# Attention maxima of two more head groups taken out of the QKV projection and into the attention's order of work

## The chip, the core and the metric

The kernel runs on one core of a Trainium2 chip. The metric is the device time of one execution in microseconds (us). A core has TensorE (PE: matmuls and transposes, PEld: its weight loads), VectorE (DVE), ScalarE (ACT), GpSimd (POOL) and SyncE (SP), each with its own queue of instructions worked off in order, and DMA queues: SP issues to the hardware queue, GpSimd to the software queue. TensorE writes to eight PSUM banks of 128 x 512 floats. Engines meet at semaphores only.

## What is computed

One "macaron" block on x of shape (1, 2048, 512): half a mixture-of-experts layer, attention, half a mixture-of-experts layer again, each with a layer norm ahead. The attention has 16 query heads and 4 key/value heads of 32, rotary positions and a causal mask:

```python
x = x + 0.5 * ffn(layernorm(x), router_w, w1, w2, w3)      # 8 experts, the best 2 of each token
x = x + attention(layernorm(x), wq, wk, wv, wo)
x = x + 0.5 * ffn(layernorm(x), router_w, w1, w2, w3)

# attention, per head
attn = where(mask, -inf, q @ k.T / sqrt(32))
out  = softmax(attn) @ v
```

The softmax here subtracts the true maximum of each row: the maximum of a query's scores over all keys that it may see has to be known before the scores are made, because it goes into the score matmul as two extra rows (96 and 97) of the query tensor `Qs`.

## The kernel before

**Stages.** First layer norm, router and experts (to about 260 us), the projection (to 414), the attention (to about 1018), then routing and experts of the second half (to 1282).

**Projection** (`project_plan` L1104, `pe_project` L1361, `dve_project` L1213, `act_project` L1298). 16 chunks `i` of 128 tokens. For a chunk, TensorE makes q, k and v (`qkv`, L1398: 24 matmuls for chunks 0 to 13, in three passes of split floats, 8 full-precision ones for the last two), transposes the next normed chunk (L1372), and transposes the rotated q and k of the chunk before into `Qs` and `Ks` (`stack`, L1415; copied by ScalarE, L1327). VectorE norms a chunk two ahead (L1228 to L1239), makes the low half of the split (L1245) and the rotation (`rope_split`, L1256 to L1271).

**Maxima.** Queries are worked on in 16 groups `G`: block `b = G // 4` of 512 queries, and four heads (`G % 4`). `tops_of(G)` (L987) lists a group's *maxima*: for each of its 4 heads and 4 times 128 queries, one per block of 512 keys up to its own block. `pe_top` (L991) makes the 128 x n scores in a PSUM bank (L997) and `dve_top` (L1001) takes the maximum of each row. For an earlier block that is one reduction over 512 columns ("full", L1010). For the own block it is `n = (c + 1) * 128` columns with the mask added ("masked", L1012). Groups 0 to 3 have 16 maxima each, all masked; groups 4 to 7 have 32, 8 to 11 48 and 12 to 15 64. The partial maxima lie in `PM`, which has room for two groups (`G % 2`).
When a group's maxima are there, a *solve* follows: VectorE reduces and splits them (`dve_found` L1017 in the projection, `dve_found_in_bank` L1034 in the attention, step "solvemax"), TensorE transposes them (`pe_found` L1053, L1059, step "found"), ScalarE copies the result to `mT` (`act_found` L1063, L1068, step "foundcopy"), and SP carries it to memory and back into rows 96 and 97 of `Qs` (`sp_found` L1084: `top<-mT` L1089, a wait for its landing, `Qs<-top` L1093). TensorE waits for that landing before the group's first score (L1628).

**Where the maxima stand.** `project_plan` puts those of groups 0 to 3 in between the projection's matmuls, from chunk 5 on: six in a chunk, four in chunk 15. Maxima, solves and stacks share a ring of three banks (5, 6, 7). VectorE reads a chunk's maxima ahead of that chunk's rotation.

**Attention** (`attend_plan` L1508). One list of steps, which every engine walks through and takes its own part of, sets the order. It runs over 160 tiles (group, 128 keys); a tile `n` has four scores `4n` to `4n + 3` (one per head, L1636), numbered 0 to 639, each followed by ScalarE's exp (L1755). Behind the last score of a tile comes the weighing of the tile before (L1648, and L1666 for the sums of exps that TensorE makes). GpSimd masks the tiles of the own block (L1814). For groups 8 and up, part of the sums of exps is made by GpSimd in `CH` (L1828) and by adding DMAs into `CD` (`CD<-P`, `CD<-CH`, L1844), which TensorE takes in at the group's end (L1657). Groups begin at scores 0, 16, 32, 48, 64, 96, 128, 160, 192, 240, 288, 336, 384, 448, 512 and 576.
The maxima of groups 4 to 15 are spread over the scores by weight: `weight` counts scores (a masked one by its share of columns), `given` counts maxima in the same measure, and maxima are put in while `given < 1.1 * weight`. A group's solve comes at the next tile end at which no sum is in the way.
Other steps stand at fixed distances from the end of a block: `xo` (SP loads the residual x, L1987), two steps `xoy` (GpSimd adds the experts' output to it by an adding DMA, `XO<-y`, L1861), and the finish of a block (projection by `WO` L1703, layer norm, store, router). They don't move with the maxima.

## Time and profile before

| | us |
|---|---|
| three runs | 1285.0, 1286.23, 1287.75 (median 1286.23) |
| the profiled execution | 1283.76 |
| its span, first to last instruction | 1282.5 |
| TensorE busy | 1197.2 (93%) |
| VectorE busy | 893.1 (70%) |
| ScalarE busy | 665.8 (52%) |
| GpSimd busy | 598.1 (47%) |

All times below are microseconds from the start of the profiled execution's span. An engine's busy time counts its own instructions, not its waits. In a timeline, the brackets at the end of a row give the idle time before the instruction and what ended it. The granted clock of TensorE is given as a share of 2.4 GHz.

### The profile page before, as it was taken

What the parts mean: (1) busy time and instruction counts of PE and PEld (TensorE: products, weight loads), DVE (VectorE), ACT (ScalarE), POOL (GpSimd) and SP (SyncE); (2) the same over time, 40 slices, a digit from 0 to 9 for tenths busy, and PEclk for the clock granted to TensorE, in tenths of its full rate; (3) what the DMA queues carried; (4) which work ended last, traced back from release to release, by engine and by line L of the source; (5) the groups of instructions that cost most, each with busy time, mean ns of one, the idle gap of its engine ahead of it and who ended that gap; (6) DMA issues with size and microseconds to landing.
All of it is one profiled execution on the core that took longest, in us unless ns stands there. A gap on an engine that the chain in (4) does not pass through costs nothing.

```text
span 1282.5 us, 22107 instructions
## 1 busy us (share of the span) xinstructions
PE 1197.2 (93%) x7413; PEld 778.6 (61%) x7413; DVE 893.1 (70%) x2100; ACT 665.8 (52%) x1321; POOL 598.1 (47%) x496
## 2 busy tenths in 40 slices
PE   4899999999998999999999999999999978999996
PEld 3678888858776554445545455545544346777774
DVE  7767777779997665476577677587763666666664
ACT  2545455436555554265466556366567853444442
POOL 4844444313210111001437556455773373888886
PEclk9899999999999999999999999999999999999999
DMA  9923333565530022013445845655743263666665
GB/s 331 365 92 108 112 111 108 172 178 108 98 60 16 21 69 35 1 59 78 98 127 138 165 100 106 192 133 146 152 100 67 84 240 72 106 100 102 101 102 79
DMA packets 68557, 148.52 MB, mean 116 GB/s; under 512 B 8832, under 2 KB 29312, under 8 KB 64448
## 3 DMA queue, kind: packets, MB, share of 16 engines
q0 software_dynamic: 35184, 93.34, 34.1%
q1 hardware_dynamic: 33264, 53.77, 12.1%
q8 instruction: 64, 1.05, 0.3%
q14 instruction: 45, 0.37, 0.1%
HBM read 81.28 MB, written 33.55 MB: 90 GB/s over the span
## 4 chain that ended last, share of the span: by engine, by line
PE 61%; DVE 15%; DMA 10%; issue 6%; POOL 4%; ACT 4%; SPq 0%; POOLq 0%; DVEq 0%; ACTq 0%
PE bank L839 10%; PE bank L1636 10%; PE bank L1648 9%; PE bank L997 8%; PE bank L862 5%; PE bank L1703 4%; PE bank L1666 4%; DMA XG<-xn,TK 3%; DMA out<-Y,DI 3%; POOL out L789 3%; DVE bank L1012 2%; DMA CD<-P 2%; DVE PM L1010 2%; PE bank L821 2%; PE bank L1398 2%
## 5 line engine op out<-in xcount | busy, mean ns | idle before, releaser
L1755 ACT ACTIVATE P<-bank 128x512 f32<-128x512 f32 (+3 forms) x640 | 304.2, 537 | 255.4 <-PE bank L1636 246.2
L1010 DVE TENSOR_REDUCE PM<-bank 128x1 f32<-128x512 f32 x384 | 252.9, 685 | 79.7 <-PE bank L997 78.9
L1636 PE MATMUL bank<-Qs,Ks 98*128 98x512 f32 (+3 forms) x640 | 242.8, 409 | 5.1 <-ACT P L1755 2.8
L997 PE MATMUL bank<-Ks,Qs 96*128 96x512 f32 (+3 forms) x640 | 233.4, 386 | 8.9 <-DVE PM L1012 5.3
L1636 PEld LDWEIGHTS bank<-Qs,Ks 98*128 98x128 f32 x640 | 117.2, 190 | 141.5 <-ACT P L1755 65.3
L1814 POOL TENSOR_SCALAR_AFFINE_SELECT P<-P 128x512 f32<-128x512 f32 x64 | 43.5, 694 | 283.4 <-ACT P L1755 283.4
L1012 DVE CUSTOM_DVE_ANT_0 bank<-bank,KB 128x128 f32<-128x128 f32 (+3 forms) x256 | 124.5, 497 | 51.4 <-PE bank L997 50.7
L1648 PE MATMUL bank<-P,V 128*32 128x512 f32 (+3 forms) x1280 | 151.3, 544 | 4.1 <-POOL P L1814 4.1
L997 PEld LDWEIGHTS bank<-Ks,Qs 96*128 96x128 f32 x640 | 121.7, 191 | 54.1 <-DVE PM L1010 17.0
L1828 POOL TENSOR_TENSOR CH<-CH,P 128x512 f32<-128x512 f32 x108 | 139.5, 1446 | 13.3 <-ACT P L1755 12.7
L789 POOL DMA_INDIRECT out<-Y,DI x78 | 126.3, 1619 | 38.2 <-issue 28.0
L951 DVE TENSOR_TENSOR DL<-W,DH 128x512 fp32r<-128x512 f32 x152 | 98.3, 688 | 41.0 <-issue 21.1
L766 POOL DMA_INDIRECT XG<-xn,TK x78 | 93.5, 1199 | 33.1 <-issue 18.0
L912 ACT CAST DH<-W 128x512 fp32r x152 | 86.7, 618 | 20.3 <-issue 20.3
L839 PE MATMUL bank<-WH,XH 128*128 x312 | 92.4, 418 | 0.9 <-issue 0.6
L839 PE MATMUL bank<-WL,XH 128*128 x312 | 85.7, 396 | 1.5 <-DVE XL L933 1.5
L839 PE MATMUL bank<-WH,XL 128*128 x312 | 85.4, 395 | 0.0
L778 POOL DMA_INDIRECT y<-Y,DI x39 | 38.7, 993 | 96.4 <-DVE Y L961 96.4
L933 DVE TENSOR_TENSOR XL<-bank,XH 128x512 fp32r<-128x512 f32 x78 | 53.9, 691 | 32.8 <-ACT XH L892 28.4
L898 ACT ACTIVATE G<-bank 128x256 f32<-128x256 f32 x78 | 29.9, 384 | 85.0 <-PE bank L839 85.0
L892 ACT CAST XH<-bank 128x512 fp32r<-128x512 f32 x78 | 45.8, 587 | 45.2 <-PE bank L821 42.1
L839 PEld LDWEIGHTS bank<-WL,XH 128*128 128x128 f32 x312 | 58.6, 188 | 16.1 <-issue 1.9
(195 smaller groups left out, 1977.7 us busy)
## 6 DMA issues: line engine op xcount, KB each, us to landing
CD<-P POOLq DMA_DIRECT2D x17, 1024.0 KB, 7.3
xn<-XN SPq DMA_DIRECT2D x8, 1024.0 KB, 6.9
WR<-L_ffn_w POOLq DMA_DIRECT2D x16, 512.0 KB, 15.1
XO<-y POOLq DMA_DIRECT2D x8, 1024.0 KB, 9.6
WR<-L_ffn_w SPq DMA_DIRECT2D x16, 512.0 KB, 7.7
CD<-P SPq DMA_DIRECT2D x7, 1024.0 KB, 5.2
CD<-CH POOLq DMA_DIRECT2D x7, 1024.0 KB, 7.5
XA<-y POOLq DMA_DIRECT2D x24, 256.0 KB, 4.1
```

Of the source, the lines that this page charges most:

```text
L766: pool.indirect_dma_start(out=x.XG[:, j % NG, :], out_offset=None, in_=g.xnd[f][:, :], in_offset=bass.IndirectOffsetOnAxis(ap=r.TK[:, j:j ...
L789: pool.indirect_dma_start(out=g.out.rearrange("t (h d) -> (t h) d", h=2), out_offset=bass.IndirectOffsetOnAxis(ap=r.DI2[:, h, j:j + 1], ax ...
L839: ins = pe.matmul(bk(g, 2 + j % 2), part[:, k * P:k * P + P], w[:, bass.ds(ev[j] * 2048 + k * 512, 512)], start=(n == 0 and k == 0), stop= ...
L912: act.copy(x.DH[:, k, :], W.W3[:, bass.ds(e * 1024 + k * 512, 512)]).then_inc(s("dh"), 1)
L951: ins = dve.tensor_tensor(x.DL[:, k, :], W.W3[:, bass.ds(e * 1024 + k * 512, 512)], DHf[:, k, :], ALU.subtract)
L997: pe.matmul(bk(g, bank)[:, 0:n], g.Qs[b][0:96, G % 4 * 4 + h, c * P:c * P + P], g.Ks[0:96, G % 4, k * BQ:k * BQ + n], start=True, stop=Tru ...
L1010: dve.tensor_reduce(dst, bk(g, bank)[:, 0:n], AX.X, ALU.max).then_inc(s(f"free{bank}"), 1)
L1012: dve.tensor_tensor_reduce(out=bk(g, bank)[:, 0:n], in0=bk(g, bank)[:, 0:n], in1=g.KB[:, CB_MASK + BQ - n:CB_MASK + BQ], scale=1.0, scalar ...
L1636: pe.matmul(bk(g, bank)[:, o:BQ], g.Ks[0:98, G % 4, k * P:k * P + P], g.Qs[G // 4][0:98, G % 4 * 4 + j, o:BQ], start=True, stop=True).then ...
L1648: ins = pe.matmul(bk(g, 3)[32 * h:32 * h + 32, o:BQ], g.V[:, k, q * HD:q * HD + HD], a.P4[buffer_of(n)][:, h, o:BQ], start=(k == 0), stop= ...
L1755: act.activation(a.P4[buffer_of(n)][:, j, o:BQ], bk(g, score_bank(g, i))[:, o:BQ], ACT.Exp, scale=scale).then_inc(s("exp"), 1)
L1828: ins = pool.tensor_tensor(to[:, h, :], two[:, h, :], one[:, h, :], ALU.add)
```

## The change

The maxima of groups 2 and 3 leave the projection: `EARLY = 2` groups are made there, three maxima per chunk (two in chunk 15) at every fourth part of its matmuls in place of every eighth. In the attention the list of maxima starts with group 2, and the spread becomes `given < 1.15 * weight + 6`: 1.15 per score, with six in advance. An assertion in the planner makes sure that a group's maxima don't overwrite the partial maxima of the group two before. Everything else stays.

```diff
+EARLY = 2
@@ project_plan
-    ahead = [key for G in range(4) for key in tops_of(G)]
+    ahead = [key for G in range(EARLY) for key in tops_of(G)]
@@
-                if (total - done) % (total // 8) == 0 and done > total // 4 and i > 4 and ahead:
+                if (total - done) % (total // 4) == 0 and done > total // 4 and i > 4 and ahead:
@@
-        if told < (64 - len(ahead)) // 16:
+        if told < (16 * EARLY - len(ahead)) // 16:
@@
-    assert told == 4
-    g.shared = [("found", G) for G in range(4)]
+    assert told == EARLY
+    g.shared = [("found", G) for G in range(EARLY)]
@@ attend_plan
-    ahead = [key for G in range(4, 4 * NB) for key in tops_of(G)]
+    ahead = [key for G in range(EARLY, 4 * NB) for key in tops_of(G)]
@@
-    told, weight, given, extra, known, solved, turned, free = 4, 0.0, 0.0, [], [], [], [], True
+    told, weight, given, extra, known, solved, turned, free = EARLY, 0.0, 0.0, [], [], [], [], True
@@
-            while ahead and given < 1.1 * weight:
+            while ahead and given < 1.15 * weight + 6:
                 key = ahead.pop(0)
+                assert key[1] < EARLY + 2 or ("solvemax", key[1] - 2) in plan, key
```

## Rows read from the trace of the kernel before

**Rows 1.** Busy time by stretch: bounds, length, then each engine's; clock; DMA.

```profile
301.50:308.45 6.95, 6.95 (x51) 6.22 (x50) 6.70 (x17) 4.52 (x12) 2.84 (x3) 1.00 0.54 105
308.45:316.41 7.96, 7.96 (x57) 6.97 (x55) 7.25 (x26) 4.51 (x12) 2.84 (x3) 1.00 0.61 116
308.45:390.28 81.83, 75.79 (x502) 64.33 (x500) 78.92 (x251) 43.27 (x95) 15.07 (x17) 1.00 0.44 80
467.40:927.08 459.68, 447.78 (x2981) 234.57 (x2977) 317.82 (x796) 245.03 (x499) 192.89 (x181) 0.99 0.47 111
710.07:713.49 3.42, 3.41 (x19) 1.35 (x20) 0.00 (x0) 0.18 (x1) 0.44 (x1) 0.50 1.12 182
```

**Rows 2.** Timeline of VectorE: start, length, instruction; a chunk, and the attention's first.

```profile
343.22 0.82 DVE L1256 TENSOR_TENSOR t<-bank,cs 128x640 f32<-128x640 f32 x1
...
348.41 0.29 DVE L1012 CUSTOM_DVE_ANT_0 bank<-bank,KB 128x128 f32<-128x128 f32 x1
...
350.88 0.69 DVE L1228 BATCH_NORM_STATS2 stA<-XA 128x6 f32<-128x512 f32 x1
...
351.93 0.82 DVE L1256 TENSOR_TENSOR t<-bank,cs 128x640 f32<-128x640 f32 x1
...
415.18 0.69 DVE L1010 TENSOR_REDUCE PM<-bank 128x1 f32<-128x512 f32 x1 [4.59 <-PE bank L997]
```

**Rows 3.** Timeline of TensorE in the attention, at six places.

```profile
422.34 0.28 PE L1636 MATMUL bank<-Qs,Ks 98*128 98x256 f32 x1
...
611.37 0.50 PE L1636 MATMUL bank<-Qs,Ks 98*128 98x512 f32 x1
...
710.08 1.51 PE L1648 MATMUL bank<-P,V 128*32 128x384 f32 x8 [1.81 <-POOL P L1814]
...
731.74 0.40 PE L997 MATMUL bank<-Ks,Qs 96*128 96x512 f32 x1
731.97 0.40 PE L1636 MATMUL bank<-Qs,Ks 98*128 98x512 f32 x1
...
734.79 0.60 PE L1059 MATMUL bank<-K,M 128*8 128x128 f32 x4
...
979.06 1.06 PE L1657 MATMUL bank<-CD,ones 128*32 128x512 f32 x8 [0.50 <-DMA CD<-CH]
```

**Rows 4.** Timeline of SP's issues to the hardware queue.

```profile
652.17 0.27 SPq L1089 DMA_DIRECT2D top<-mT  x1
656.45 0.22 SPq L1093 DMA_DIRECT2D Qs<-top  x1
...
681.42 0.38 SPq L362 DMA_DIRECT2D xn<-XN  x1
...
692.22 0.29 SPq L1089 DMA_DIRECT2D top<-mT  x1
693.68 0.25 SPq L1093 DMA_DIRECT2D Qs<-top  x1
694.03 0.39 SPq L1987 DMA_DIRECT2D XO<-L_attn_x  x1
...
906.57 0.29 SPq L1089 DMA_DIRECT2D top<-mT  x1
911.78 0.24 SPq L1093 DMA_DIRECT2D Qs<-top  x1
```

**Rows 5.** Timeline of GpSimd's issues to the software queue.

```profile
606.58 1.29 POOL L1861 DMA_DIRECT2D XO<-y  x1 [0.43 <-issue]
...
649.32 0.87 POOL L1844 DMA_DIRECT2D CD<-P  x1 [4.89 <-ACT P L1755]
...
707.10 0.86 POOL L1844 DMA_DIRECT2D CD<-CH  x1 [4.34 <-DMA CD<-P]
...
903.87 2.09 POOL L1861 DMA_DIRECT2D XO<-y  x1
```

**Rows 6.** Chain of the work that ended last, in order of time: start, length, what.

```profile
693.93 12.63 DMA CD<-P
```

## Prediction

> **What bounds the kernel now.** I read the stretches of time first, because the change takes work out of one stage (the projection, up to 414 us) and puts it into another (the attention, 414 to 1018 us), so what counts is what each stage is short of. A chunk of the projection without a maximum takes 6.95 us, and TensorE is busy for all of it; the first chunk with six maxima takes 7.96 us, again with TensorE full [rows 1]. The nine chunks with six maxima together take 81.83 us, or 9.09 each, but there TensorE is busy for only 75.79 us of it and VectorE for 78.92: the later of these chunks are VectorE's [rows 1]. The timeline of VectorE confirms it: from one chunk's first rotation product (343.22) to the next one's (351.93) are 8.71 us without an idle time, of which six maxima take 350.88 - 348.41 = 2.47 us [rows 2]. Without them VectorE's own chunk is 6.24 us, less than TensorE's 6.95. In the attention the roles are turned: from 467.40 to 927.08 TensorE is busy for 447.78 of 459.68 us, VectorE for 317.82 [rows 1]. So a maximum that leaves the projection gives back VectorE time that was on the path, and in the attention it costs TensorE time that is on the path. Last I looked at what is not steady: transfers and waits around the attention's groups, in the timelines of SP and GpSimd [rows 4, 5], since the new plan moves every later group's maxima by some scores.
>
> **Projection, what is removed.** 32 of 64 maxima go (groups 2 and 3, all masked ones, of 128 to 512 columns), and two of the four small solves that end a group's maxima. Three per chunk stay in place of six. TensorE's price of one, from the first chunk, where nothing waits: (7.96 - 6.95) / 6 = 0.17 us [rows 1]. VectorE's price: 2.47 / 6 = 0.41 us for the six narrower ones of that chunk [rows 2]; over all four widths I take 0.44, an estimate. A chunk then needs 6.95 + 3 x 0.17 = 7.46 us of TensorE and 6.24 + 3 x 0.44 = 7.56 us of VectorE, so both are nearly equal and I take 7.56. Nine chunks make 68.0 us, plus 0.5 for the one solve that still falls in them: 68.5 in place of 81.83, a gain of 13.3. The last two chunks lose three and two maxima, 5 x 0.17 = 0.8. Together **-14.1 us**. From both sides: if the two engines wait for each other now and then, and a chunk takes 7.8, the gain is 12; if VectorE's surplus is carried along to the end and TensorE sets 7.46, it is 15. The tail of the stage (the last rotation, its transposes) has the same instructions as before.
>
> **Attention, what is added.** The planner's arithmetic, followed, gives 28 maxima between scores 0 and 15 (14 before), 16, 13 and 15 in the next three groups (14, 13, 14), 24 more than before in groups 4 to 13 (15 full ones, 9 masked), and 28 in place of 36 in group 14; the last is placed after score 533, not 541.
> Group 0: twelve maxima stand behind score 0, and 24 behind the first eight scores. TensorE can be only three banks ahead of VectorE, so VectorE sets the pace: from 415.18 [rows 2], 24 x 0.44 = 10.6 us, to 425.8; then the small solve (0.6) and its transposes, 0.60 by their row at 734.79 [rows 3], so that score 9 starts at 427.0 where it started at 422.34 [rows 3]. That is +4.6. The half clock with which the attention starts lies under VectorE's work then.
> Groups 1 to 3: one full maximum fewer and four masked more, and one solve more. A full one costs TensorE 731.97 - 731.74 = 0.23 us in the steady part [rows 3]; for a masked one I take 0.19, between the projection's 0.17 and that. A solve costs up to 0.60 of transposes, partly overlapped, and something of a wait for VectorE's three small operations; I take 0.8 in all (0.4 to 1.2). Sum +1.3.
> Groups 4 to 13: 15 x 0.23 + 9 x 0.19 = +5.2. VectorE has the room (317.82 of 459.68 us busy [rows 1]), so I add nothing for it; the bound above is 24 x 0.44 = 10.6.
> Group 14: eight maxima fewer would be worth 1.8 us, but the transfer that carries GpSimd's share of the sums already comes last there: TensorE waited 0.50 us for it at 979.06 [rows 3]. Its chain starts with exps of this group that the change moves by a few tenths. I count nothing back (-1.8 to +0.4) and take +0.3.
> Sum of the four: 4.6 + 1.3 + 5.2 + 0.3 = **+11.4 us**, 8 to 15.
>
> **Attention, what is moved.** Two pieces hang on the order of the queues. *Group 8's maxima.* Their copy by ScalarE and their two small transfers (to memory and back into Qs) stood behind score 177 and now stand behind score 185; group 8's first score is 192, at 611.37 [rows 3]. GpSimd's adding transfer of the residual (the second XO<-y of block 1) stands behind score 185 as well, just ahead, and was issued at 606.58 [rows 5]. A small transfer behind such a one waits for it: issued at 652.17 behind CD<-P of 649.32 it let the second go only at 656.45, and issued at 906.57 behind XO<-y of 903.87 only at 911.78; with nothing in the way the step takes 693.68 - 692.22 = 1.46 us [rows 4, 5]. In both loaded cases the step ended 7.1 and 7.9 us after the large one's issue. So for group 8: 606.58 + 7.1 to 7.9 = 613.7 to 614.5, and one more step of 1.46: 615.1 to 616.0. TensorE stands before score 192 until then, 3.8 to 4.6 us, and all that it has queued (scores, maxima, weighing) stands behind it, with ScalarE and VectorE waiting. After an idle 1.81 us at 710.08 the clock stood at half for 3.42 us [rows 1, 3], so I add 1.5 for the clock: **+5.7 us** (0 to 8). The other groups keep time: group 4 is the next tightest, seven scores for some 3.5 us of copy and transfers.
> The Trainium skill (DMA: Bandwidth & Descriptors, Queues, rings and completion order) says that an engine takes turns between queues packet by packet, draining a whole packet before it switches. By that rule a small transfer would wait for a part of the large one only; if that part is short, the term falls to about nothing and the sum to some 1280.5. The rows above show waits of 2.8 and 3.8 us.
> *Block 2's residual.* SP took the transfers of group 10's maxima (behind score 265) ahead of the load XO<-L_attn_x (behind 266); now that copy stands behind 269 and the load goes first. The load doesn't wait for a score, so it leaves right behind the store of XN, issued at 681.42, and not at 694.03 [rows 4]. There it ran together with CD<-P of 693.93, which took 12.63 us [rows 6]; GpSimd waited 4.34 us for it at 707.10 [rows 5], the mask behind it came late, TensorE idled 1.81 us at 710.08 [rows 3] and had the half clock until 713.49 [rows 1]. Without the collision that is 1.81 + about 1.4 (3.42 us at half speed, partly spent on work that waits anyway) = **-3.2 us**. The load then meets the CD<-P ahead of that one, issued about when XN is stored; nobody needs it before the next is issued at 693.93, so I count no new wait (up to +2).
>
> **Sum.** -14.1 + 11.4 + 5.7 - 3.2 = -0.2 us. The profiled execution took 1283.76 us (span 1282.5 and 1.3 around it), so 1283.6 by this; the median of the three runs is 1286.23, 2.5 above it, so the forecast is 1286.0.
>
> **The rivals.**
> *1. Group 8's maxima land in time* (faster). The small transfers get through between the packets, or GpSimd's large one leaves later than they do. For it: the margin is decided by which of two issues, some 2 us apart, comes first. Against: both loaded cases, with 2.85 and 2.70 us between the two issues [rows 4, 5]. Time: 1286.0 - 5.7 = 1280.3.
> *2. The collision moves but doesn't go* (slower). The residual's load, now right behind the store of XN (681.42 [rows 4]), lies on top of that and of the CD<-P of the same moment; if that CD<-P takes over 12 us too, an exp that needs its buffer and the next CD<-P wait for it, and the -3.2 turns into +1 or so: 1290.2. It decides from a landing later than 693.93 on. For it: three megabytes at once. Against: two at once took 12.63 us [rows 6], and half a microsecond less than that is still in time; the store also begins first.
> *3. The burst costs more* (slower). With TensorE waiting for VectorE in the first 10 us, its clock may stay at half beyond them, and groups 0 to 3 lose 2 to 3 us more: 1288.5.
> *4. The maxima hide in the attention* (faster). Steps in which TensorE waits for ScalarE could take some of the 24 masked or full ones; by a third of 11.4: 1282.2.
> That the change doesn't do what it says I leave out: every maximum is in a list, and both lists come from the same function.
>
> **How the numbers follow.** A measurement of this kernel tells about 0.2% from no change, 2.6 us. Forecast 0.40 (1283.5 to 1288.8), rival 1 0.22, rival 2 0.16, rival 3 0.12, rival 4 0.10. Faster by over 0.2% (below 1283.6): rivals 1 and 4 and a little of the forecast, 0.34. Slower (above 1288.8): rivals 2, most of 3, and a little of the forecast, 0.28. Same 0.38. The range reaches to rivals 1 and 2 with the projection's bounds: 1280.0 to 1291.5.
>
> **What the new profile would show.** Chunks of 7.5 to 7.6 us in the projection, the first score near 400; group 0 some 4.5 us longer, with TensorE waiting for PM; an idle time of 4 us before the score that opens group 8, with a top<-mT whose second half leaves late; no idle time at the mask in group 9, and XO<-L_attn_x issued right behind xn<-XN; the rest, from the experts on, unchanged. I am wrong if a projection chunk stays above 8 us, or if the attention grows by less than 9 or more than 20 us.

## The result, and the profile after

The changed kernel takes 1299.02 us (median of four runs, 1297.82 to 1300.71), the kernel before on the same chip 1285.62 (four runs, 1283.95 to 1287.75): a ratio of 1.010, 95% interval 1.007 to 1.013. It is slower by 13 us. The forecast was 1286.0, the range ended at 1291.5, and slower had the smallest of the three chances. The profiled execution took 1298.21 us, with a span of 1297.0; before it was 1283.76 and 1282.5.

Each run below has a label, e1 to e15. The table holds the lengths of the stages of all runs below, read from the starts of the first projection matmul, of the scores that open a group, and of score 639. "G4-6" is groups 4 to 6 together. What lies after score 639 (the last tile and the second half's experts) has the same work in all of them, and took between 269.1 and 274.1 us in the profiled executions, in no order that follows the edits; so single steps are judged by the stages, and a kernel by its interval.

```
                     projection   G0  G1-3   G4-6  G7-8    G9  G10-13   G14   G15  attention
before                    140.4  12.2  40.9  109.9  87.4  50.3   212.1  49.9  36.4   599.1
after                     127.0  21.7  42.2  112.3  97.6  48.6   214.7  51.1  36.4   624.5
e1_ramp                   125.9  16.2  44.3  112.4  99.0  50.0   215.1  52.2  36.0   625.3
e2_late_add               125.8  21.8  42.2  112.4  90.5  48.5   214.7  51.1  36.3   617.5
e3_warm                   125.7  21.9  42.2  114.0  96.0  48.5   214.7  52.4  36.0   625.6
e4_before_load_first      141.8  11.2  40.9  109.9  87.4  47.3   212.2  49.9  36.5   595.2
e5_ramp_late_add          125.7  18.5  44.3  112.4  90.6  48.4   214.7  51.1  36.3   616.3
e6_fill                   125.7  18.4  42.2  112.4  96.7  48.5   214.6  52.4  36.0   621.2
e7_xo_back                127.1  21.8  42.2  113.9  96.1  47.2   214.6  51.1  36.5   623.4
e8_before_spread          140.4  17.5  40.8  110.1  90.2  47.1   214.6  48.9  36.4   605.5
e9_all                    125.7  16.1  44.3  112.4  90.6  47.4   214.7  52.3  36.0   613.8
e10_three_early           134.7  17.0  41.4  113.6  90.6  48.9   213.9  50.4  36.3   612.0
e11_pe_twice              127.2  21.5  42.8  113.8  92.1  48.7   217.6  52.4  37.2   626.2
e12_dve_twice             127.0  21.5  44.4  122.0  93.3  50.4   222.7  51.8  36.3   642.4
e13_dve_short             125.7  21.7  42.1  110.1  89.9  48.4   213.1  50.9  36.3   612.4
e14_both_short            126.9  21.5  42.0  109.4  88.9  50.0   211.5  50.9  36.5   610.5
e15_load_first_again      140.4  12.2  40.9  109.9  87.4  47.1   212.1  49.9  36.5   596.0
```

The projection gave back 13.4 us, near the 14.1 of the sum, and the attention took 25.4 where the sum had 13.9. The stretches of the changed kernel that answer to [rows 1] (bounds, length, busy time of PE, PEld, DVE, ACT, POOL, granted clock, DMA share, GB/s) are a chunk without a maximum, the first with three, the nine, the attention up to score 9, the first 9.4 us of group 8, and groups 4 to 13:

```profile
303.58:310.49 6.91, 6.91 (x52) 6.20 (x49) 6.66 (x17) 4.51 (x12) 2.83 (x3) 1.00 0.55 109
310.49:317.84 7.35, 7.35 (x55) 6.61 (x52) 5.97 (x20) 4.50 (x12) 2.84 (x3) 1.00 0.64 119
310.49:378.44 67.95, 67.73 (x467) 59.98 (x465) 64.53 (x190) 42.93 (x93) 15.30 (x17) 1.00 0.52 95
402.95:419.48 16.53, 15.67 (x54) 9.39 (x54) 12.05 (x51) 4.51 (x9) 1.27 (x2) 0.59 0.18 65
617.50:626.90 9.40, 9.40 (x37) 6.86 (x38) 5.97 (x13) 5.85 (x10) 0.00 (x0) 0.50 0.28 112
466.85:940.00 473.15, 453.92 (x3004) 240.68 (x3000) 329.05 (x828) 247.29 (x499) 192.71 (x181) 0.99 0.46 108
```

The nine chunks took 67.95 us, 7.55 each, with TensorE busy for all but 0.22: VectorE, at 64.53 us, is no longer what sets them. The two other short stretches stand out by the clock: 0.59 and 0.50, where 0.50 is its lower level, 1.2 GHz. TensorE's timeline shows what they consist of (start, length, instruction, idle time before it and what ended that):

```profile
404.07 0.71 PE L998 MATMUL bank<-Ks,Qs 96*128 96x512 f32 x2 [0.24 <-DVE PM L1013]
...
415.45 1.94 PE L1650 MATMUL bank<-P,V 128*32 128x512 f32 x8
417.16 1.81 PE L1668 MATMUL bank<-P,ones 128*32 128x512 f32 x8
...
419.12 0.60 PE L1060 MATMUL bank<-K,M 128*8 128x128 f32 x4
...
617.50 0.80 PE L1638 MATMUL bank<-Qs,Ks 98*128 98x512 f32 x1 [4.09 <-DMA Qs<-top]
...
709.66 0.50 PE L998 MATMUL bank<-Ks,Qs 96*128 96x512 f32 x1 [1.53 <-ACT mT L1069]
```

In the first stretch, the weighing and the sums at 415.45 and 417.16 take nearly twice as long as the same instructions at full speed (1.06 and 1.07 us in group 14 of the kernel before). At 617.50 stands the idle time that the prediction had put at 3.8 to 4.6 us. The one at 709.66, in group 9, it had not. VectorE in the burst, its first two rounds of four masked maxima and its last:

```profile
403.66 0.30 DVE L1013 CUSTOM_DVE_ANT_0 bank<-bank,KB 128x128 f32<-128x128 f32 x1 [5.76 <-PE bank L998]
...
405.43 0.33 DVE L1013 CUSTOM_DVE_ANT_0 bank<-bank,KB 128x128 f32<-128x128 f32 x1
...
407.48 0.33 DVE L1013 CUSTOM_DVE_ANT_0 bank<-bank,KB 128x128 f32<-128x128 f32 x1
...
416.26 0.22 DVE L1044 TENSOR_REDUCE bank<-PM 128x16 f32<-128x16 f32 x1
```

The first round takes 405.43 - 403.66 = 1.77 us, 0.44 for each maximum as forecast. The second takes 2.05, since now VectorE waits for TensorE at times too: 24 maxima took 416.26 - 403.66 = 12.6 us, not 10.6.

### The profile page after: what moved, and what is told of

It is laid out like the page before. It is cut to its first block, busy times and chain, and to the rows that moved or that the text cites. A ratio compares the mean times of both kernels' runs of the same rounds, so it can differ in the third digit from the quotient of the medians.

```text
span 1297.0 us, 22109 instructions
## 1 busy us (share of the span) xinstructions
PE 1209.3 (93%) x7413; PEld 787.1 (61%) x7413; DVE 890.7 (69%) x2100; ACT 669.3 (52%) x1321; POOL 597.5 (46%) x496
## 3 DMA queue, kind: packets, MB, share of 16 engines
q1 hardware_dynamic: 33264, 53.77, 12.2%
## 4 chain that ended last, share of the span: by engine, by line
PE 63%; DVE 13%; DMA 10%; issue 6%; POOL 5%; ACT 3%; SPq 0%; POOLq 0%; DVEq 0%; ACTq 0%
PE bank L840 10%; PE bank L1638 9%; PE bank L998 8%; PE bank L1650 8%; PE bank L863 6%; PE bank L1705 4%; PE bank L1668 4%; DMA out<-Y,DI 3%; PE bank L1399 3%; DMA XG<-xn,TK 3%; DVE PM L1011 3%; POOL out L790 3%; PE bank L822 2%; DVE bank L1013 2%; PE bank L1416 2%
## 5 line engine op out<-in xcount | busy, mean ns | idle before, releaser
L998 PEld LDWEIGHTS bank<-Ks,Qs 96*128 96x128 f32 x640 | 124.3, 195 | 50.5 <-DVE PM L1011 16.3
L1830 POOL TENSOR_TENSOR CH<-CH,P 128x512 f32<-128x512 f32 x108 | 139.2, 1440 | 13.4 <-ACT P L1757 12.8
L790 POOL DMA_INDIRECT out<-Y,DI x78 | 125.7, 1612 | 39.3 <-issue 29.4
L1668 PE MATMUL bank<-P,ones 128*32 128x512 f32 (+3 forms) x664 | 67.2, 476 | 2.4 <-DVE PM L1011 2.1
## 6 DMA issues: line engine op xcount, KB each, us to landing
WR<-L_ffn_w POOLq DMA_DIRECT2D x16, 512.0 KB, 14.5
```

The source lines that it names most:

```text
L790: pool.indirect_dma_start(out=g.out.rearrange("t (h d) -> (t h) d", h=2), out_offset=bass.IndirectOffsetOnAxis(ap=r.DI2[:, h, j:j + 1], ax ...
L998: pe.matmul(bk(g, bank)[:, 0:n], g.Qs[b][0:96, G % 4 * 4 + h, c * P:c * P + P], g.Ks[0:96, G % 4, k * BQ:k * BQ + n], start=True, stop=Tru ...
L1668: ins = pe.matmul(bk(g, 4)[32 * h:32 * h + 32, o:BQ], g.ones[:], a.P4[buffer_of(n)][:, h, o:BQ], start=fresh, stop=last)
L1830: ins = pool.tensor_tensor(to[:, h, :], two[:, h, :], one[:, h, :], ALU.add)
```

## Group 8: the transfer behind the adding DMA

SP's issues, then GpSimd's, around the opening of group 8 in the changed kernel:

```profile
610.33 0.29 SPq L1090 DMA_DIRECT2D top<-mT  x1
615.39 0.25 SPq L1094 DMA_DIRECT2D Qs<-top  x1
```

```profile
607.94 1.29 POOL L1863 DMA_DIRECT2D XO<-y  x1 [0.43 <-issue]
```

The small transfer left 2.39 us behind the adding one and its step took 5.06 us, as in the loaded cases of [rows 4, 5]. The experiment takes the adding transfer out of its way:

```diff
-        put(at + 22, ("xoy", b, 1))
+        put(at + (32 if b == 1 else 22), ("xoy", b, 1))
```

> The changed kernel, but the second XO<-y of block 1 stands ten scores later (195 in place of 185), behind the transfers of group 8's maxima. Theory 1 (that adding transfer holds the small ones up): top<-mT takes 1.5 us and not 5.07, the idle 4.09 us before group 8 goes and the half clock of 10.24 us with it, and groups 7 and 8 take 97.6 less 8 to 9 us. Theory 2 (seven scores are too few for copy and transfers anyway, or the clock falls there for another reason): at least 1.5 us of idle time or a half clock stays, and the gain is below 5.

It took 1291.31 us, a ratio to the kernel before of 1.0016 (0.9992 to 1.0040). Its SP issues, then GpSimd's:

```profile
607.75 0.29 SPq L1090 DMA_DIRECT2D top<-mT  x1
609.21 0.25 SPq L1094 DMA_DIRECT2D Qs<-top  x1
```

```profile
611.28 1.29 POOL L1863 DMA_DIRECT2D XO<-y  x1 [0.43 <-issue]
```

TensorE's row of score 192 there:

```profile
611.04 0.50 PE L1638 MATMUL bank<-Qs,Ks 98*128 98x512 f32 x1 [0.20 <-DMA Qs<-top]
```

The step takes 1.46 us, TensorE is idle for only 0.20 us before score 192 and keeps full speed, and groups 7 and 8 take 90.5 us in place of 97.6: theory 1, though it had 8 to 9 us. So this wait cost **7.1 us**: 4.09 of idle time before group 8, and the rest, by subtraction, from the half clock that came with it, 10.2 us long. In four other runs with the same wait (3.7 to 4.3 us) that half clock lasted 6.8 (e3, e6, e7) or 13.7 us (e1), and group 8 took 58.0, 58.1, 57.9 and 60.5 us against 59.3 here: 3.4 us of half clock more or less went with 1.2 us.

## Group 0: the burst and the clock

Four experiments on the changed kernel and one on the kernel before. **e1** builds the advance up slowly, and e5 adds the later adding transfer to it:

```diff
-            while ahead and given < 1.15 * weight + 6:
+            while ahead and given < 1.15 * weight + min(6, at / 8):
```

> The changed kernel, but its six maxima in advance are given out over the first 48 scores (min(6, score / 8) in place of 6); from there on its plan is the same. Theory 1 (the burst at the attention's start leaves TensorE waiting for VectorE, and its clock stays at half): the half clock of 13.65 us shrinks to 3.4 to 7, and groups 0 and 1 take 31 to 33 us in place of 36.6, so the kernel gains about 4 to 5. Theory 2 (the moved maxima themselves are dear, wherever they stand): groups 0 and 1 stay within 1 us of 36.6 apart from the five maxima that leave group 0 for groups 1 and 2.

> The changed kernel with both repairs: the advance of six maxima is only built up over the first 48 scores (min(6, at / 8)), and block 1's second adding transfer of the residual is put behind score 202 in place of 185 (the copy of group 8's maxima stands behind 185 or later). Nothing is left out. Theory 1 (the two causes are separate and add up): group 0 16 us and groups 0 to 3 together 60.5 (63.9 in the changed kernel), groups 7 and 8 together 90.5 (97.6), no idle time before the score that opens group 8; the attention 624.5 - 3.4 - 7.1 = 614, the kernel some 10 us under the changed one, 1288 to 1290, so within 0.3% of the kernel before. Theory 2 (what is taken away comes back further on, since the plan's maxima are only moved): the attention stays above 618 and the time above 1292.

**e3** puts 12 products that nobody reads ahead of the last transposes of the projection, where TensorE waits for the last rotation:

```diff
     def stack(i):
+        if i == NT - 1:
+            for _ in range(12):
+                pe.matmul(bk(g, 4), g.KB[:, CB_ONE:CB_ONE + P], g.KB[:, 0:512], start=True, stop=True)
```

> The changed kernel with twelve idle matmuls into bank 4 while TensorE waits for the last rotation (2.67 us), ahead of the projection's last transposes. Theory 1 (the idle time before the attention sets the clock down, and the burst only keeps it there): no half clock between 398 and 419, the last transposes take 2.6 us in place of 4.05, group 0 takes 15 to 17 us in place of 21.7, total gain 5 to 7. Theory 2 (the burst's waits for VectorE set the clock down by themselves): the transposes gain 1.5 us, and group 0 still shows a half clock of several us and stays above 19.

**e6** puts such a product into the burst itself:

```diff
             pe_top(g, step)
+            if step[1] == 2:
+                pe.matmul(bk(g, 4), g.KB[:, CB_ONE:CB_ONE + P], g.KB[:, 0:512], start=True, stop=True)
```

> The changed kernel, with one more product of 512 columns behind each of group 2's 16 maxima, written to a bank of the sums that the first weighing overwrites; nothing is left out. In group 0 TensorE then does work where it waited for VectorE. Theory 1 (TensorE's clock stands at half in the burst because it waits for VectorE there; the clock is the price above VectorE's own 24 x 0.44 us): the half clock of 13.7 us from 405 on shrinks to under 7 us, the burst keeps VectorE's pace, the weighing and the sums behind it run at full clock (about 1.0 us in place of 1.9 each), and group 0 takes 19 to 20 us in place of 21.7, in spite of the added products. Theory 2 (the clock falls whatever TensorE does there, or the added products take longer than the waits that they fill): the half clock stays at 10 us or more and group 0 takes 22 us or more.

**e8** is the kernel before with the new spread alone (`given < 1.15 * weight + 6` in place of `given < 1.1 * weight`):

> The kernel before, with the new spread alone: its 36 maxima of groups 4 on are still spread after four groups were told in the projection, but by 1.15 per score with six in advance (18 maxima behind the first eight scores in place of 10, 22 in group 0 in place of 14; group 8's copy stands behind score 169, well ahead of the adding transfer at 185). Nothing is left out. Theory 1 (the burst itself costs, by VectorE's pace and by the clock that falls with it): the half clock after score 0 lasts 10 us or more in place of 3.4, group 0 takes 16 to 17.5 us in place of 12.2, where eight more full maxima at 0.25 us would give 14.2. Group 8 has no idle time ahead of it and takes 53 to 54 us. The kernel is 5 to 10 us slower than before, about half of it given back in group 14, which has 6 maxima in place of 36. Theory 2 (the burst needs masked maxima of moved groups to hurt, or costs by its count alone): group 0 at 14.2 us or less and the half clock at 3.4 us.

Stretches from score 0 on: e6 up to score 9 and up to group 1, then group 0 of e1, of e5, and of e8, each from its own trace:

```profile
398.83:412.02 13.19, 13.00 (x69) 7.27 (x70) 11.47 (x51) 4.32 (x9) 1.27 (x2) 1.00 0.25 81
398.83:417.19 18.36, 17.59 (x112) 9.70 (x112) 13.63 (x59) 6.95 (x17) 2.46 (x4) 1.00 0.19 60
```

```profile
398.77:414.94 16.17, 14.78 (x91) 8.14 (x91) 11.21 (x49) 7.01 (x17) 2.55 (x4) 0.89 0.22 67
```

```profile
399.62:418.14 18.52, 17.49 (x91) 9.86 (x91) 11.58 (x49) 7.17 (x17) 2.55 (x4) 0.72 0.19 59
```

```profile
414.53:432.02 17.49, 16.94 (x87) 10.27 (x87) 12.11 (x33) 6.65 (x16) 2.47 (x4) 0.71 0.18 61
```

- e6: with TensorE given work in its waits, the clock stays at 1.00, though 16 products are added. Score 9 comes 13.19 us behind score 0; in the changed kernel it comes after 16.53, and the prediction had 12.7. The 24 maxima take VectorE 10.98 us there, where the prediction had 10.6 and the changed kernel 12.6. So of the burst's excess **3.3 us is the clock's**, and VectorE's pace was forecast nearly right. (1294.65 us, 1.0076, 1.0044 to 1.0107.)
- e3: work ahead of the projection's last wait doesn't help. The half clock came just the same, from 401.9 for 13.7 us, and group 0 took 21.9: it is in the burst that TensorE has to have work. (1300.3 us, two runs.)
- e1 and e5 have the same plan in group 0, and 16.17 and 18.52 us. The difference is the half clock alone: 3.4 us long in one and 10.2 in the other. Why it lasted longer in one, these runs don't show. What the slower advance saves in group 0 it gives back in part in groups 1 to 3 (44.3 for 42.2 us). e1 took 1298.67 us (1.0079, 1.0021 to 1.0138): its 3.4 us in groups 0 to 3 went again in groups 7 and 8 (half clock 13.7 us and not 10.2), in group 9 (3.4 us of half clock that the changed kernel's trace doesn't have), and in group 14, where TensorE waited 2.62 us for GpSimd's mask and the changed kernel 0.72. e5 took 1291.11 us (1.0045, 1.0026 to 1.0064), its attention 616.3 us where theory 1 said 614; the 2.3 missing are group 0's clock.
- e8: the new spread alone makes group 0 of the kernel before 5.3 us longer, with the half clock at 10.2 in place of 3.4 us, and the kernel takes 1295.22 us (1.0071, 1.0048 to 1.0094). The new spread is a cost of its own, without a single maximum moved out of the projection: the attention takes 605.5 us for 599.1. Part of the 5.3 us is the work of eight more maxima in group 0, four full and four masked (the expectation took eight full ones, at 2 us). Group 8 took 55.2 us, not the 53 to 54 expected. Group 14, with 6 maxima in place of 36, gave back only 1.1 us, not the half that was expected: there GpSimd's additions set the end (below). With group 10's copy at score 253 there, its group 9 takes 47.1 us, without the wait at the mask too.

## Group 9: block 2's residual

Undone in the changed kernel (e7), and done alone in the kernel before (e4, and e15 with more rounds):

```diff
-        put(at, ("xo", b))
+        put(at + (4 if b == 2 else 0), ("xo", b))    # e7, on the changed kernel
+        put(at - (4 if b == 2 else 0), ("xo", b))    # e4 and e15, on the kernel before
```

> The kernel before with nothing changed but the place of block 2's residual load: four scores earlier (262), so that SP issues it ahead of the transfers of group 10's maxima. Theory 1 (it only moves the collision): the idle 1.81 us at the mask and the half clock at 710 go (-3.2), the CD<-P that is issued with the store of XN takes 13 to 14 us and holds up an exp and TensorE by about 2.3, so group 9 takes 49 to 50 us in place of 50.3. Theory 2 (as I predicted: a free gain): group 9 takes 47 us.

> The kernel before with block 2's load of the residual four scores earlier, the same as in the earlier run, to tell 0.2%. Nothing is left out. Theory 1 (its trace's gain of 3 us in group 9 is a gain of the kernel): 1283 to 1285 where the kernel before has 1286 to 1287, a ratio of 0.997 to 0.999. Theory 2 (executions differ by as much in their experts' stage): a ratio of 0.999 to 1.001.

> The changed kernel with block 2's load of the residual put four scores later, so that the two small transfers of group 10's maxima go ahead of it again, as in the kernel before. Nothing is left out. Theory 1 (the queue order of this load sets what group 9 waits for): the idle time of 1.5 us ahead of the score that opens the last tile of group 9 goes, CD<-P and the load run together a step later, TensorE waits 1.5 to 2 us at the mask of tile 280 and the half clock comes back for 3.4 us there; group 9 takes 50 to 52 us in place of 48.6, and the kernel is 1.5 to 3 us slower than the changed one. Theory 2 (the collision's place doesn't matter to group 9): group 9 stays within 48.3 to 49.0 us and the time is the same.

In the kernel before, the load ahead of the small transfers shortens group 9 from 50.3 to 47.3 and 47.1 us, the 3.2 of the sum (theory 2 of e4); the kernel as a whole gives 1285.6 (1.0002, 0.9975 to 1.0029) and 1284.36 us against 1288.27 (0.9984, 0.9960 to 1.0007). That is a gain in the trace and none that the times can tell from no change. In the changed kernel the same order costs: e7, with the load behind again, has a *shorter* group 9 (47.2 for 48.6 us), and no wait at the mask. Its SP issues, then those of the changed kernel, and then a part of the changed kernel's chain of the work that ended last (start, length, what):

```profile
691.31 0.38 SPq L363 DMA_DIRECT2D xn<-XN  x1
705.52 0.29 SPq L1090 DMA_DIRECT2D top<-mT  x1
709.95 0.25 SPq L1094 DMA_DIRECT2D Qs<-top  x1
710.30 0.40 SPq L1989 DMA_DIRECT2D XO<-L_attn_x  x1
```

```profile
693.97 0.38 SPq L363 DMA_DIRECT2D xn<-XN  x1
694.46 0.44 SPq L1989 DMA_DIRECT2D XO<-L_attn_x  x1
```

```profile
694.07 13.91 DMA CD<-P
...
708.08 0.07 ACT P L1757
...
708.58 0.59 ACT P L1757
709.17 0.45 ACT mT L1069
709.62 0.04 issue
709.66 0.50 PE bank L998
```

The load did meet the CD<-P ahead of the critical one, as the prediction said; but that one then took 13.91 us, ScalarE's exp waited for its buffer, and behind the exp on ScalarE's queue stood the copy `mT` for which TensorE waits. In e7 the load leaves at 710.30, and no CD<-P near it is waited for. Neither theory of e7 held (the first had the sign wrong, the second no change). The collision's first place costs 1.4 us here, and its second, where the kernel before lost 3, is empty in the new plan since the copy has moved from score 265 to 269. The kernel as a whole took 1296.66 us (1.0095, 1.0059 to 1.0132).

That the order on ScalarE's queue makes the difference shows in e4, which has the same collision. ScalarE's rows there:

```profile
691.27 0.56 ACT L1068 CAST mT<-bank 8x512 fp32r<-8x512 f32 x1
...
695.25 1.08 ACT L1755 ACTIVATE P<-bank 128x512 f32<-128x512 f32 x2 [1.97 <-DMA CD<-P]
```

An exp waits for a CD<-P there too, 1.97 us, but `mT` was copied 4 us ahead of it, and TensorE lost nothing. In e2, which has the changed kernel's order, the wait for `mT` is there again (1.56 us at 700.01).

## What a maximum costs the attention

Groups 4 to 13 got 23 maxima more, 14 full and 9 masked (508 in the trace, 485 before; the prediction counted 24). Without group 8's wait (e2) they are 466.08 us long, where before they had 459.68, and group 9 had lost its 3 us of wait on the way: so 6.4 + 3.1 = 9.5 us for 23 maxima and what they disturb (1.4 of it the new wait in group 9), not 5.2. Four runs price TensorE's and VectorE's part apart; all have the later adding transfer, so e2 is what they are held against. The same 48 full maxima, four in each of groups 4 to 15, are made twice by one engine, or over 128 of their 512 columns:

```diff
+    if k == 0 and c == 0 and b:      # e11: the product twice
+        pe.matmul(bk(g, bank)[:, 0:n], ..., start=True, stop=True)
```
```diff
+        if k == 0 and c == 0:        # e12: the reduction twice
+            dve.tensor_reduce(dst, bk(g, bank)[:, 0:n], AX.X, ALU.max).then_inc(g.dv.sem, 1)
+            dve.wait_ge(g.dv.sem, g.dv.up())
```
```diff
-        dve.tensor_reduce(dst, bk(g, bank)[:, 0:n], AX.X, ALU.max)...     # e13; e14 cuts the product too
+        dve.tensor_reduce(dst, bk(g, bank)[:, 0:(P if k == 0 and c == 0 else n)], AX.X, ALU.max)...
```

> The changed kernel with the later adding transfer (as in the run that had only that), where TensorE makes 48 of the full maxima's products twice, four in each of groups 4 to 15, into the same bank; VectorE has nothing more to do. Nothing is left out. Theory 1 (a maximum's place in the attention costs TensorE's 0.23 us and that is all on the path): 48 x 0.23 = 11.0 us more attention than without the doubling (617.5), 628 to 629. Theory 2 (steps in which TensorE waits take some of it): 4 to 9 us more.

> The same 48 maxima, but VectorE reduces each of them twice (and waits for its own first one); TensorE has nothing more to do. Nothing is left out. It adds some 48 x 0.75 = 36 us of VectorE work between 430 and 960 us. Theory 1 (VectorE has the room, as the prediction had it): 0 to 3 us more attention than without the doubling (617.5). Theory 2 (VectorE's part of a maximum reaches the path where its work is bunched, which is why a moved maximum cost 0.33 us and not 0.22): 4 to 10 us more, spread over the groups, with the most in those that have row statistics.

> The changed kernel with the later adding transfer, in which VectorE reduces only 128 of the 512 columns of 48 full maxima, the same four in each of groups 4 to 15 that were doubled before; TensorE makes them whole. Left out is the maximum over the other 384 columns of these. It takes some 48 x 0.4 = 19 us from VectorE and nothing from TensorE. Theory 1 (VectorE's part of a maximum is on the path already at its present size, where its work is bunched): the attention 3 to 10 us under 617.5. Theory 2 (VectorE has room as it is, and only the 36 us added before went beyond it): 0 to 2 us under.

> The same, and the product of these 48 maxima is made over 128 columns only as well. Left out is the same part of the maxima, with its products. It takes 48 x 0.17 = 8 us from TensorE beside VectorE's 19. Theory 1 (both are on the path, in turn): the attention another 5 to 8 us under the run with the short reduction alone, 10 to 16 in all. Theory 2 (TensorE alone sets it): 6 to 9 us under 617.5 in all, and all of it from this step.

Attention against e2's 617.5 us: e11 +8.7 (1300.8 us in all), e12 +24.9 (1316.27), e13 -5.1 (1286.63), e14 -7.0 (1284.77; -8.5 without the 1.5 that a half clock at 695.6 put back into group 9).

- e11: a doubled product costs 0.18 us (theory 2, not the 0.23 of the sum).
- e12: a doubled reduction costs 0.52, far above both theories. It is 0.69 us long and waits for its twin. Part of the 0.52 is the clock: this trace has 20.5 us of half clock in groups 4 to 13, and e2's, e11's and e13's have none. By the prices above that is an estimated 5 to 7 of the 24.9 us.
- e13: a reduction over a quarter of its columns gives back 0.11 (theory 1).
- e14: the shorter products gave 0.07 more each, less than either theory had for that step. The total lies where theory 2 had it, but theory 2 gave all of it to the products, and e13 shows that most of it is VectorE's.

So VectorE's part of a maximum is on the path already, and the more so the more of it there is. The view of waits over groups 4 to 13 (instruction, what it waited for, us in total, times, longest) shows where. The kernel before, e2, and e12:

```profile
PEld bank L997 <- DVE PM L1010: 12.2, 41, 0.5
...
PEld bank L1059 <- DVE M L1050: 3.7, 5, 1.4
...
PE bank L1059 <- DVE M L1050: 1.7, 3, 1.0
...
PE bank L1666 <- DVE PM L1010: 0.6, 1, 0.6
```

```profile
PEld bank L998 <- DVE PM L1011: 13.8, 46, 0.5
...
PEld bank L1060 <- DVE M L1051: 6.1, 7, 1.3
...
PE bank L1060 <- DVE M L1051: 3.3, 5, 0.9
...
PE bank L1668 <- DVE PM L1011: 2.1, 2, 1.5
```

```profile
PEld bank L998 <- DVE PM L1014: 24.2, 59, 1.2
...
PEld bank L1063 <- DVE M L1054: 9.5, 8, 2.1
...
PE bank L998 <- DVE PM L1014: 6.9, 12, 1.0
PE bank L1063 <- DVE M L1054: 6.6, 7, 1.7
```

TensorE waits for a bank that VectorE hasn't read yet (PM), and at each solve for VectorE to get through what stands ahead of M. New is a wait of 1.46 us behind a reduction, at 871.54 in the changed kernel (score 435; e2's is the 1.5 in its last row). The first two rows stood in the trace of before as well, at 12.2 and 3.7 us: VectorE was idle for 31% of the time and yet late in places. One place is the tile of score 224, where the solve of group 9 now falls: it took 3.25 us before, 5.16 after, 5.89 in e12 and 4.76 in e13, so part of it follows VectorE's load.

Group 14 (+1.1 us, with eight maxima fewer) has a limit of its own. GpSimd adds without a pause from its start to near its end; in the kernel before its first CD<-P leaves 15.3 us behind the group's first score, and in e5 15.9. The maxima stand a little denser in the group's first tiles (28 over 22 scores, before 36 over 30), which could hold up the exps that it adds; that isn't shown. The maxima that are missing further on give nothing back, since TensorE then waits for GpSimd's mask, 1.06 us before, 2.22 in e5:

```profile
971.17 1.06 PE L1648 MATMUL bank<-P,V 128*32 128x512 f32 x8 [1.06 <-POOL P L1814]
```

```profile
973.67 1.07 PE L1650 MATMUL bank<-P,V 128*32 128x512 f32 x8 [2.22 <-POOL P L1816]
```

In the changed kernel and in e2 that wait is 0.72 and 0.45 us, with a half clock of 3.4 us in this group and other waits ahead of it, and the group is 51.1 us long in all three.

## The whole with its repairs, and half of it

e9 has all repairs together, with the filling products only up to the first weighing:

```diff
+        put(at + (4 if b == 2 else 0), ("xo", b))
+        put(at + (32 if b == 1 else 22), ("xoy", b, 1))
+            while ahead and given < 1.15 * weight + min(6, at / 8):
+            if not getattr(g, "weighed", False):      # behind pe_top; set by the first weighing
+                pe.matmul(bk(g, 4), g.KB[:, CB_ONE:CB_ONE + P], g.KB[:, 0:512], start=True, stop=True)
```

> The changed kernel with all four repairs: the advance built up over 48 scores (min(6, at / 8)), block 1's second adding transfer ten scores later, block 2's load of the residual four scores later, and a product of 512 columns behind each maximum up to the first weighing (written to the bank that the first sums overwrite), so that TensorE is busy in the burst. Nothing is left out. Theory 1 (four separate causes that add up): no half clock behind score 0 and group 0 16 us; groups 7 and 8 together 90.5; group 9 47.2; the attention 611 to 614 us, and the kernel 1283 to 1287, level with the kernel before or up to 0.3% under it. Theory 2 (the repairs disturb each other, as the plan moves with each): the attention 616 or more and the kernel 1289 or more.

e10 moves group 3's maxima alone:

```diff
-EARLY = 2
+EARLY = 3
-                if (total - done) % (total // 4) == 0 and done > total // 4 and i > 4 and ahead:
+                if (total - done) % (total // (4 if total == 24 else 8)) == 0 and done > total // 4 - (total == 24) and i > 4 and ahead:
-        put(at, ("xo", b))
+        put(at - (4 if b == 2 else 0), ("xo", b))
-            while ahead and given < 1.15 * weight + 6:
+            while ahead and given < 1.13 * weight + min(4, at / 8):
```

> Half of the change: only group 3's maxima are moved (three groups are told in the projection, four maxima per chunk), spread by 1.13 per score with an advance of min(4, at / 8), and block 2's load four scores earlier. Nothing is left out. Theory 1 (a chunk pays for its maxima by VectorE above four of them, 6.24 + 4 x 0.44 = 8.0 us, and the attention pays 0.3 to 0.35 us for each of 16, without a burst): chunks of 7.8 to 8.1, the projection 131 to 132 us, group 0 14 to 15, the attention 602 to 606, and the kernel 2 to 6 us under the kernel before. Theory 2 (each moved maximum costs the attention what it gives back to the projection, whatever the dose): the attention 608 or more and no gain.

e9: 1288.06 us against 1286.98, a ratio of 1.0008 (0.9991 to 1.0026). Theory 1 held for the stages: group 0 took 16.05 us at full clock, groups 7 and 8 90.6, group 9 47.4, the attention 613.8 (611 to 614 expected); the kernel's 1288.06 lies 1 us above its 1283 to 1287. Projection and attention together are 125.7 + 613.8 = 739.5 us, and before they were 140.4 + 599.1 = 739.5. The four repairs take 10.7 off the attention's 25.4 us; 14.7 are left, as much as the projection gave. But that compares unlike things: the kernel before has a wait of 3 us in group 9, which e9 is rid of, and which e4 and e15 take from the kernel before without moving a maximum. Against e15's attention (596.0) the 32 maxima cost 17.8 us, 0.56 each, and the projection had them at 14.7, 0.46 each.

e10: 1291.14 us (1.0042, 1.0020 to 1.0064), theory 2. Two stretches of its trace: the nine chunks, and the half clock around score 0 (at 408.12):

```profile
310.26:383.50 73.24, 71.59 (x473) 61.15 (x471) 70.07 (x210) 42.48 (x92) 15.43 (x17) 1.00 0.48 81
401.50:418.60 17.10, 14.88 (x55) 11.11 (x59) 8.19 (x32) 9.44 (x17) 1.27 (x2) 0.50 0.20 65
```

A chunk with four maxima takes 8.14 us, near the 8.0 expected, but the last two chunks have six each, the clock falls already at the projection's end and stays at half for 17.1 us, and TensorE waits 2.19 us for a reduction just ahead of score 140 (558.66). Against e15, which has the same place of the load, the projection gives 5.7 us and the attention takes 16.0. No kernel here beats the kernel before by more than its interval; e15 is the nearest.

## Why the prediction was wrong

| step | forecast | measured |
|---|---|---|
| projection | -14.1 | -13.4 (-14.5 to -14.7 in seven other runs) |
| group 0 | +4.6 | +9.5 |
| groups 1 to 3 | +1.3 | +1.3 |
| group 8's wait | +5.7 | +7.1 |
| group 9: residual | -3.2 | -1.7 |
| other groups from 4 to 13 | +5.2 | +8.1 |
| groups 14 and 15 | +0.3 | +1.1 |
| sum | -0.2 | +12.0 |

The profiled execution is longer by 14.45 us; the 2.4 beyond the sum lie ahead of the projection (2.1) and behind score 639, where no instruction was changed.

- **Projection: size right, mechanism in part.** The prediction took 7.56 us per chunk from VectorE, with TensorE at 7.46; measured were 7.55, but TensorE was busy for 67.73 of the 67.95 us and VectorE for 64.53, so TensorE sets the chunks now. In the changed kernel's profiled execution a half clock of 3.4 us fell on the last transposes, and from them to score 0 it took 1.3 us longer than in runs without it.
- **Group 0: the step "the half clock ... lies under VectorE's work then" failed**, and it is two thirds of the miss in this term. VectorE set the pace as said, but TensorE, waiting for it inside the burst, had the half clock for 13.7 us and was then late for VectorE, and the weighing and the sums, which wait for nobody, take some 1.6 us more. e6 shows 3.3 us for it. That is rival 3's mechanism; its price was 2 to 3 us and its chance 0.12. The remaining 1.6 us are 0.5 ahead of score 9 (13.19 us in e6, not 12.7) and 1.0 behind it: from there to group 1 it took 5.16 us (419.48 to 424.64) where it had been 4.18, which the sum left out.
- **Group 8: mechanism and idle time right** (4.09 us in 3.8 to 4.6), found from two like cases of [rows 4, 5]. The clock was mis-sized: 3.4 us at half were counted, at 1.5 us, and there were 10.2, at 3.0. By the rule of the Trainium skill (DMA: Bandwidth & Descriptors, Queues, rings and completion order), that an engine takes turns packet by packet, I had held open that the wait goes; the trace shows a step of 5.06 us beside one of 1.46 without the adding transfer, so here the turns, if they are taken, don't shield a small transfer.
- **Group 9: the wait at the mask went as said, and "I count no new wait (up to +2)" failed by 1.4 us.** That a CD<-P lands in time for its next issue was examined for GpSimd's queue, not for ScalarE's, where an exp needs the same buffer and a copy for TensorE stands behind it.
- **Groups 4 to 13: the step "VectorE has the room, so I add nothing for it" failed.** It was argued from 317.82 of 459.68 us busy. e13 refutes it: with less work for VectorE alone the attention is 5.1 us shorter; e12 does so from the other side. The count was off by one as well: the prediction's own numbers (32 moved, +14 in group 0, +3 in the next three, -8 in group 14) leave 23, not 24, 14 full and 9 masked, so its sum should have read +4.9. What part of the 8.1 us each wait has isn't shown.
- **Group 14: sign right, size short.** In e5's trace, which has the same plan there, GpSimd's first CD<-P is 0.6 us later in the group and the wait at its mask 1.16 us longer; in the changed kernel's trace other waits stand in that one's place. Why the additions start later is open.
- **The range** left out the sum of these: the text had an upper end for each term (the projection's -12, 15 for what the attention adds, 8 for group 8, a new wait of 2 on the -3.2, and 3 for the clock), and together they reach -12 + 15 + 8 - 1.2 + 3 = +12.8, but the range went to one rival at a time. Nor does it come out of the rivals as said: with the projection's bounds they reach from 1279.4 to 1292.3, not from 1280.0 to 1291.5. All the misses but that of groups 1 to 3, which is nothing, have one sign: in each TensorE waited, or had the half clock, for longer than was counted.

On the clock, the Trainium skill (TensorE: Matmul & The Clock Gate, Terms) puts the penalty at the time spent throttled times one half. For the burst that would be 6.8 us; measured were 3.3 for 13.7 us, 2.4 for 6.8 more (e5 against e1), and 1.2 for 3.4 in group 8. The rule is an upper bound here; that part of the work at half clock waits for other engines anyway would explain it, and isn't shown.

## What to carry to other kernels

Don't take room on an engine from its share of busy time: look in the view of waits for rows in which the bound engine already waits for it (12.2 and 3.7 us here), because those grew when work was added (to 24.2 and 9.5 in e12). Work that is moved costs what it costs where it arrives: 32 maxima were worth 14.7 us in the projection and, with all repairs, 17.8 in the attention, and on top came what the move stirred up (a burst with the clock at half, a small transfer behind an adding one, a new collision). A repair that helps the kernel before by itself, as the load's place does in its trace, belongs on both sides of the comparison. When several terms err in one direction for one reason, the range has to hold their sum, not the largest.

## What the runs showed of the hardware

- Waits of TensorE of only 0.2 to 0.3 us, one behind every one to four products, went with a granted clock at half for 13.7 us (e3 and e2 as well), and work that nobody reads, put in those waits, kept it at full (e6, e9). The same plan had it at half for 3.4 us once and 10.2 us another time (e1, e5).
- A hardware-queue transfer of a few rows takes 1.46 us from issue to the issue that waits for its landing; behind an adding transfer of the software queue issued 2.4 us earlier it took 5.06, and 4.7 to 5.3 us in the other runs with that order (e1, e3, e6, e7).
- Group lengths of one plan repeat within 0.2 us from one execution to the next where the clock is the same, while what lies after score 639 took 274.1 us in e4 and 269.4 in e15, which are the same kernel: a part of 3 us can be read from the trace and not from the times.
